# The last layer's row maximum with its sign turned, the score scale in the rotation table, and VectorE's steps in other slots

## The reference, cut to what matters

```python
q = (query @ Wq).reshape(bsz, tgt_len, 2 * H, D)      # H = 16, D = 8: 32 sub-heads of 8
k = (query @ Wk).reshape(bsz, tgt_len, 2 * H, D)
v = (query @ Wv).reshape(bsz, tgt_len, H, 2, D)
q = apply_rotary_interleaved(q, cos, sin)
k = apply_rotary_interleaved(k, cos, sin)
s = jnp.einsum('bthd,bshd->bhts', q, k) * scale       # scale = D ** -0.5
s = jnp.where(mask, s, NEG)
a = jax.nn.softmax(s, axis=-1)
...
attn_freq = f1 - lambda_full * f2                     # low-pass filter over time
attn = attn * jax.lax.rsqrt(jnp.mean(attn * attn, axis=-1, keepdims=True) + EPS) * rms_weight
...
x = x + _L1_attn_ref(_layernorm(x), ...)
x = x + _L1_xattn_ref(_layernorm(x), ctx_2048, ...)   # here: add one row per sequence, norm, gamma, beta
x = x + _L1_ffn_ref(_layernorm(x), ...)               # ternary quantization, then one product
```

## Time and profile before

| | us |
|---|---|
| median of 3 runs (1388.69 to 1391.48) | 1388.76 |
| the profiled execution | 1389.57 |
| its span | 1387.8 |
| DVE busy in the span | 935.5 |
| from the first exponential of the last layer (1005.13) to the end of the span | 382.7 |

### The profile page before, as it was taken

The page is one execution under the profiler, slowest core; times in us unless marked ns, Lnnn a source line. Parts: engine busy times, 40 slices in busy tenths (PEclk is TensorE's granted clock), DMA queues, the critical chain, the costliest instruction groups (busy, mean ns, idle before and its releaser), DMA issues.

```text
span 1387.8 us, 25403 instructions
## 1 busy us (share of the span) xinstructions
PE 1123.2 (81%) x8276; PEld 970.0 (70%) x8338; DVE 935.5 (67%) x2266; ACT 564.2 (41%) x1990; POOL 535.1 (39%) x575
## 2 busy tenths in 40 slices
PE   6999898888889898955786899996478877777753
PEld 6898898888888787954685699885356655555532
DVE  5756768587867778688663367563367787788753
ACT  5534243332333242413242233332176775667531
POOL 1112122233424343243331465667124355554454
PEclk9999999999999999987798899998689998899765
DMA  5320000101010101015465777675200000000000
GB/s 173 123 69 16 17 24 5 55 13 53 20 47 22 44 24 32 29 35 180 150 182 141 174 131 111 103 116 81 68 17 9 23 17 24 16 17 9 16 18 21
DMA packets 72663, 84.13 MB, mean 61 GB/s; under 512 B 11720, under 2 KB 62632, under 8 KB 72408
## 3 DMA queue, kind: packets, MB, share of 16 engines
q1 hardware_dynamic: 55608, 60.74, 14.7%
q0 software_dynamic: 14592, 19.41, 8.5%
q10 hardware_dynamic: 2336, 2.36, 0.5%
HBM read 49.90 MB, written 32.58 MB: 59 GB/s over the span
## 4 chain that ended last, share of the span: by engine, by line
PE 44%; DVE 27%; DMA 10%; issue 8%; ACT 5%; POOL 4%; SPq 1%; DVEq 0%; POOLq 0%; ACTq 0%
PE bank L514 5%; PE bank L515 5%; PE bank L516 5%; PE bank L1503 4%; PE bank L1969 3%; PE bank L575 3%; DMA xs<-xg,slot 2%; DMA yt<-y_sb,xe 2%; PE bank L1982 2%; PE bank L551 2%; DMA x_sh<-y_sb,xe 2%; DVE k_st L2275 2%; DMA x_sh<-x2e 2%; ACT ex L2101 2%; PE bank L1447 2%
## 5 line engine op out<-in xcount | busy, mean ns | idle before, releaser
L740 ACT ACTIVATE qk<-bank,b_col 128x256 f32<-128x256 f32 x256 | 107.3, 471 | 249.6 <-PE bank L516 247.2
L2101 ACT ACTIVATE ex<-bank,nmx 128x64 f32<-128x64 f32 x512 | 153.4, 337 | 83.3 <-DVE nmx L2285 77.1
L414 POOL TENSOR_TENSOR probs<-shifted,rowinv 64x512 f32<-64x512 f32 x64 | 71.0, 1109 | 275.9 <-DVE rowinv L911 206.7
L514 PE MATMUL bank<-xt_hi,w_hi 128*128 128x256 f32 x512 | 155.4, 304 | 5.3 <-DVE w_lo L875 4.9
L515 PE MATMUL bank<-xt_lo,w_hi 128*128 128x256 f32 x512 | 149.6, 292 | 0.0
L516 PE MATMUL bank<-xt_hi,w_lo 128*128 128x256 f32 x512 | 149.2, 291 | 0.0
L1867 POOL TENSOR_TENSOR k_bd<-k_st,bd_mask 128x512 f32<-128x512 f32 x64 | 67.9, 1063 | 166.0 <-PE bank L1982 147.2
L2101 ACT ACTIVATION_READ_ACCUMULATOR ex<-bank,nmx 128x1 f32 x512 | 117.5, 230 | 0.0
L514 PEld LDWEIGHTS bank<-xt_hi,w_hi 128*128 128x128 f32 x512 | 103.4, 202 | 6.4 <-issue 4.5
L1553 ACT ACTIVATE act_e<-bank 128x176 f32<-128x176 f32 x112 | 35.5, 317 | 172.4 <-PE bank L1449 171.0
L756 ACT ACTIVATE at_hi<-bank,b_col 128x256 fp32r<-128x256 f32 x128 | 53.8, 472 | 126.1 <-PE bank L575 126.1
(11 more groups left out here) (298 smaller groups left out, 3254.3 us busy)
## 6 DMA issues: line engine op xcount, KB each, us to landing
xe<-xs SPq DMA_DIRECT2D x80, 136.0 KB
e_stage<-w_up SPq DMA_DIRECT2D x18, 352.0 KB
terms<-w_qkv SPq DMA_DIRECT2D x12, 512.0 KB, 5.0
down<-w_down SPq DMA_DIRECT2D x16, 176.0 KB
xs<-zero SPq DMA_DIRECT2D x17, 136.0 KB, 1.8
yt<-zero ACTq DMA_DIRECT2D x1, 2176.0 KB, 8.2
xin<-x SPq DMA_DIRECT2D x8, 256.0 KB, 3.0
terms<-w_o SPq DMA_DIRECT2D x4, 512.0 KB, 4.8
```

The costliest lines, as they stand in the source:

```text
L414: pool.tensor_tensor(probs[r, :, SEQ * s:SEQ * s + SEQ], expd[r, :, :], rowinv[r, :].unsqueeze(2).broadcast_to([SEQ, TC * GH, SEQ]), ALU.m ...
L514: nc.tensor.matmul(out, l_hi, r_hi, start=start, stop=False, skip_group_check=True)
L740: ins = nc.scalar.activation(qk[:, par, hh, o, :], p_proj[hh % 2][:, o * TOK:o * TOK + TOK], ACT.Identity, bias=b_col[:, o, h:h + 1])
L2101: ins = nc.scalar.activation(ex[:, g % 2, j, :], p_s[g % 2][:, j * SEQ:j * SEQ + SEQ], ACT.Exp, bias=nmx[:, g % 2, j:j + 1], scale=SCALE1, ...
```

## The change

Five things are done, all in the last layer but one instruction:

1. `row_max` takes the maximum with its sign turned in the reduction and writes nmx directly; rmx and the multiply by minus the scale are gone, and with them the wait between the two.
2. The scale stands in a second rotation table, rope_q = scale x rope_t, used for the queries. It is computed once on DVE, in round 28 of the constants, inside the expert layer. The exponentials lose their scale operand.
3. ACT copies the exponentials in u = 1, 3, 4, 5 and 7, DVE in u = 0, 2 and 6: one copy per block goes from DVE to ACT.
4. On DVE `comb(t+2)` goes from u = 2 to u = 0, `norm1(t+2)` from u = 6 to u = 1, and `wout(t-2)` stands behind the row_max of its slot and not ahead of it.
5. On POOL `power(1, t+2)` goes from u = 7 to u = 3.

```diff
             for o in range(2):
                 ins = nc.vector.tensor_tensor(
                     dst[:, o], src[:, o],
-                    rope_t[:, o, :].unsqueeze(1).broadcast_to([P, BB, SEQ]), ALU.mult)
+                    (rope_t if which else rope_q)[:, o, :].unsqueeze(1).broadcast_to([P, BB, SEQ]), ALU.mult)
...
-            ch(nc.vector.tensor_reduce(rmx[:, g % 2, :], p, AX.X, ALU.max))
-            nc.vector.tensor_scalar(nmx[:, g % 2, :], rmx[:, g % 2, :], -SCALE1, None, ALU.mult
+            nc.vector.tensor_reduce(nmx[:, g % 2, :], p, AX.X, ALU.max, negate=True
                                     ).then_inc(S["mx_ready"], 1)
...
                 ins = nc.scalar.activation(ex[:, g % 2, j, :], p_s[g % 2][:, j * SEQ:j * SEQ + SEQ], ACT.Exp,
-                                           bias=nmx[:, g % 2, j:j + 1], scale=SCALE1,
+                                           bias=nmx[:, g % 2, j:j + 1],
...
-            nc.scalar.activation(et[:, g % 2, :], p_e[g % 2][:, :], ACT.Copy).then_inc(S["e_read1"], 1)
+            nc.scalar.activation(et[:, g % 2, :], p_e[g % 2][:, :], ACT.Copy
+                                 ).then_inc(S[f"e_read{g % 2}"], 1)
...
-                if units(g - 2) and g % 2:
+                if units(g - 2) and u not in (0, 2, 6):
                     copy_exp(g - 2)
...
                 ch(nc.vector.tensor_reduce(lam_s[:, 0:2], lam[:, 0:2, :], AX.X, ALU.add))
+                ch(nc.vector.tensor_scalar(rope_q[:, :, :], rope_t[:, :, :], SCALE1, None, ALU.mult))
...
-                if units(g - 2) and g % 2 == 0:
+                if units(g - 2) and u in (0, 2, 6):
                     copy_exp(g - 2)
-                if u == 1 and blocks(t - 2):
-                    wout(t - 2)
...
                 if u == 1 and blocks(t - 2):
+                    wout(t - 2)
                     z_stats(t - 2)
+                if u == 1 and blocks(t + 2):
+                    norm1(t + 2)
...
-                if u == 2 and blocks(t + 2):
+                if u == 0 and blocks(t + 2):
                     comb(t + 2)
-                if u == 6 and blocks(t + 2):
-                    norm1(t + 2)
...
-                if u == 7 and blocks(t + 2):
+                if u == 3 and blocks(t + 2):
                     power(1, t + 2)
```

More of the change, by code:

```diff
@@ L167, in memory @@
                 ("sum_rows", [BATCH, DIM]), ("sum_c0", [P, KC, BATCH]), ("sum_c1", [P, KC, BATCH]),
-                ("sum_t", [BATCH, 1]), ("rope_t", [P, 2, SEQ]), ("circ", [P, P]),
+                ("sum_t", [BATCH, 1]), ("rope_t", [P, 2, SEQ]), ("rope_q", [P, 2, SEQ]), ("circ", [P, P]),
                 ("bd_mask", [P, USUB]), ("rms_c", [P, 1]), ("lam", [P, 4, D1]), ("lam_s", [P, 4]),
@@ L171, in memory @@
                 ("nmv", [P, 5, TC, 2]), ("nrs", [P, 5, TC]), ("nbias", [P, 5, TC]), ("zero_c", [P, TC]),
-                ("rmx", [P, 2, USUB]), ("nmx", [P, 2, USUB]), ("rs", [P, 2, TC, SUB]), ("rin", [P, TC, SUB]), ("ss", [P, 2 * H1]), ("ssr", [P, 2 * H1]),
+                ("nmx", [P, 2, USUB]), ("rs", [P, 2, TC, SUB]), ("rin", [P, TC, SUB]), ("ss", [P, 2 * H1]), ("ssr", [P, 2 * H1]),
                 ("keep1", [P, 2 * H1]), ("v_w", [P, KC, DIM]))
@@ L1710, in layer1 @@
     sum_blk = summary.rearrange("(i c s) d -> i s c d", c=TC, s=2)
-    (qk_w, v_w, wo_w, ffn_w, ident, ident16, mask1, rope_t, bd_mask, circ, gamma_r, beta_r, lam, lam_s,
+    (qk_w, v_w, wo_w, ffn_w, ident, ident16, mask1, rope_t, rope_q, bd_mask, circ, gamma_r, beta_r, lam, lam_s,
      neg_lam, rms_c, half1, sum_b, sum_t, sum_rows, wq_a, wq_b, wq_r) = (
-        T[n] for n in """qk_w v_w wo_w ffn_w ident ident16 mask1 rope_t bd_mask circ gamma_r beta_r lam
+        T[n] for n in """qk_w v_w wo_w ffn_w ident ident16 mask1 rope_t rope_q bd_mask circ gamma_r beta_r lam
         lam_s neg_lam rms_c half1 sum_b sum_t sum_rows wq_a wq_b wq_r""".split())
@@ L1719, in layer1 @@
      d sq xa hi_q""".split())
-    nstat, nmv, nrs, nbias, rmx, nmx, rs, rin, ss, ssr, keep1 = (
-        T[n] for n in "nstat nmv nrs nbias rmx nmx rs rin ss ssr keep1".split())
+    nstat, nmv, nrs, nbias, nmx, rs, rin, ss, ssr, keep1 = (
+        T[n] for n in "nstat nmv nrs nbias nmx rs rin ss ssr keep1".split())
     bank = T["banks"]
```

## The result

| | before | after |
|---|---|---|
| median of 12 runs each, same chip | 1391.83 (1385.94 to 1399.79) | 1380.04 (1368.62 to 1384.69) |
| profiled execution (span) | 1389.57 (1387.8) | 1381.82 (1380.0) |
| first exponential of unit 0 to that of unit 63 | 322.75 | 312.38 |

The changed kernel is faster: ratio 0.9892, 95% interval 0.9867 to 0.9917, that is 15 us less (11.6 to 18.5); the medians differ by 11.8. The forecast, 1383.6 from a sum of 5.2, has the sign and too small a size. That 1380.04 lies in its range says little: the kernel before has a median of 1391.83 here, 3.1 above the 1388.76 that the forecast started from.

The account below looks back on a forecast made before the run. No engine was full; a chain of waits through ACT, PE and DVE was taken to set a block's length. Terms 1.4 + 1.0 + 1.2 + 0.2 + 1.35 = 5.15 us, off 1388.76, gave 1383.6; range 1378.0 to 1387.8.

Parts of the forecast that it names:

- The fill: Ahead of block 0: norm 1 leaves (1.21 us) and the maximum is ready 0.20 sooner; gain 1.4.
- The back of block 0: End of block 0: norm 1 goes, nmx shrinks, d loses a collision, rin meets a k_bd; gain 1.0, bounds 0.3 and 2.2.
- The ends of blocks 1 to 5: Removing norm 1 there gains 0.0, as waits replace it; nmx leaves 4 x 0.2 + 0.4 = 1.2 us.
- The comparison of blocks 5 and 6: From k_st to nmx, block 5 with norm 1 takes 5.46 us, block 6 without 5.50: norm 1's 1.21 become a wait.
- with it PE's ffn and the last rotation ... so that is hidden: Ends of blocks 1 to 5: the u = 5 maximum comes 0.2 us sooner, but k_st's waits for POOL hide that.
- The fronts: Stretch from a block's first exponentials to PE's first query product; the forecast's sum had no term for it.
- Block 7: Units 58 to 60 start sooner, rms gains 1.9 less 0.5 for ACT's new copy: 1.35 us, bounds 0 and 2.5.
- The costs put at nothing: rope_q (some 0.2 us), ACT's fourth copy, DVE's moved steps, POOL's power and the sign-turned reduction: covered by waits or unchanged.
- Of the rivals, the first: The ports don't take norm 1's time back: blocks 1 to 5 save some 1.0 us more each, 1378.6; chance 0.17.

Follow-up runs that it names:

- the maximum first: A block's last maximum put ahead of rms_end and scale(t, 0): on the kernel before, median 1364.6 us, loop 299.50; on the changed kernel, 1358.3, loop 289.67.

## Why the prediction was wrong

*The fill* (1.4): right. From the last rotation to the first exponentials it is 4.20 before, 4.00 with edits 1 and 2 alone or with norm 1 taken back, and 2.79 in the changed kernel: 0.20 and 1.21. The whole stage from `comb` to them was 0.7 longer than before, since two of PE's products there ran at the low clock (2.1 more). With either order this stage differs between executions (26.4 to 32.1 over all traces), so a trace of each doesn't tell whether the change has a part in that.

*The back of block 0* (1.0, bounds 0.3 and 2.2): 1.61. d fell from 1.31 to 0.42, 0.9 less, and rin took 0.94 where 0.23 is free, 0.7 more. With the norm's 1.2 that makes 1.4, as the run with norm 1 back has it, and the nmx adds 0.2. The prediction's own items give 1.21 + 0.2 + 0.96 - 0.9 = 1.5 even with rin's wait at its upper end; the 1.0 stood below them without a reason.

*The ends of blocks 1 to 5* (1.2 together): for blocks 3 to 5 the step held: norm 1 taken back changed nothing in blocks 3 and 5, and 0.16 in block 4. The comparison of blocks 5 and 6 before was the right one: att 1.46, ssr 0.61, the k_bd in one piece, and 0.17 to 0.20 less at equal clock. It failed for blocks 1 and 2, 0.67 and 1.62 for my 0.2 and 0.4. The words "with it PE's ffn and the last rotation ... so that is hidden" were carried over from block 5, where ffn exists and the rotation waits for PE. Blocks 1 and 2 have no ffn, all their maxima count (0.52 and 0.65), and in block 2 the norm counts (0.96). There ssr took 1.27 before, so the collisions were paid already: the four products ssr, att, rin and d took 3.31 before and 3.51 after. In block 1 they took 1.59 and 2.67, which takes the norm back. Of block 5's change of -0.89 the clock in ffn is -1.20; of block 4's 1.44 it is 1.25.

*The fronts*: the sum had no term for them. They gave 4.0 of the 10.4 in the traces, the largest of what was missed. I took PE's stretch from the exponentials to the values as of fixed length, though the windows of rows 2 already had clocks of 0.93 and 0.89 in neighbouring blocks. The wait that the change shortens is one in which PE is idle, and in block 3 PE came out of the shorter one at the high clock. This was followed row by row in blocks 1 and 3 only; for the others PE's work at the low clock accounts for the length, to a tenth in blocks 0 to 3. Why the clock was high there is not shown, nor that another execution of the two kernels would give 4.0 again: with the maximum first in both, the fronts differ by 0.1 in sum. The 12 runs of each kernel say only that the whole is worth 11 to 15.

*Block 7* (1.35, bounds 0 and 2.5): right, 1.54, by the rms 1.5 sooner. Behind PE's projection it is 1.63: the place of wout and norm 1.34 and the maximum 0.76, together 2.1 for my 1.9, and the moved copy -0.47 for my -0.5. (1.9 - 0.5 is 1.4; the prediction wrote 1.35.) The projection itself took 0.1 longer, by the clock.

*The costs put at nothing*: rope_q took 0.23 us; the rotations still wait for PE (20.4 us over 13 waits between 1049 and 1304). The reduction with its sign turned takes 683 ns on the mean of 64, the plain one 0.68.

The terms that were mis-sized: fronts 4.0 for 0, ends of blocks 1 to 5 3.0 for 1.2, end of block 0 1.6 for 1.0. What the traces show at equal clock comes to 7.7: fill 1.4, block 0 1.6, blocks 1 and 2 0.7 and 1.6, blocks 3 to 6 0.2 each, block 7 1.6. Of the 2.5 by which that is more than the forecast, 2.3 lie in blocks 0 to 2; the rest of what was missed goes with the clock. Of the rivals, the first has the nearest time (1378.6), but its reason fell: collisions take the norm back in blocks 1 and 3 to 5.

## What to carry to other kernels

When two neighbouring stages differ by one step and have the same length, look for the wait that takes the step's place: it tells both that removing the step elsewhere brings nothing, and what to move instead (here one maximum ahead of two small steps, worth 22.7 us of the loop where the five edits were worth 10.4). Carry such a comparison only to stages that wait for the same engine. And where a shorter wait is one of PE's, add a term for the clock and widen the range to its side: parts that bring 3.5, 4.2 and -1.1 alone brought 10.4 together. Read the price of an edit where PE's clock is the same in both traces or plays no part: behind the projection of block 7 the moved copy cost 0.47 to 0.49 in three pairs of traces, while the whole block said 0.0, 0.56 and 0.9.
